# Expert stage of a Perceiver block: activation transposes three turns, second products four turns behind the row transposes, weights asked for three turns ahead

## What is computed

```python
logits = x @ router_w.T + expert_bias
top_w, top_idx = jax.lax.top_k(sigmoid(logits), 8)        # 160 experts, 2048 tokens
top_w = top_w / (sum(top_w) + 1e-09) * 2.5
h1 = silu(einsum('th,eih->eti', x, w_gate))               # w_gate 160 x 128 x 256
routed = einsum('eti,ehi->th', h1 * combine.T, w_down)    # w_down 160 x 256 x 128
x = x + routed + silu(x @ w_gate_shared.T) @ w_down_shared.T
```

## Time and profile before

| | |
|---|---|
| median of 3 runs | 1385.31 us (1382.23 to 1386.63) |
| the profiled execution | 1384.27 us |
| its span, first to last instruction | 1381.1 us |
| mean granted clock of TensorE over the span | 0.954 |
| expert stage, first weight request to last scatter | 1005.9 to 1329.2 us of the span |

### The profile page before, as it was taken

How to read it: one execution, slowest core, us unless ns; L and a number is a source line. 1 busy time by engine, 2 the same in 40 slices (tenths; PEclk the granted TensorE clock), 3 DMA queues, 4 the chain that set the end, 5 groups by cost and what they waited for, 6 DMA issues and landing times.

```text
span 1381.1 us, 34814 instructions
## 1 busy us (share of the span) xinstructions
PE 1244.3 (90%) x11693; PEld 897.9 (65%) x11693; DVE 946.3 (69%) x2728; ACT 605.4 (44%) x1761; POOL 548.0 (40%) x717
## 2 busy tenths in 40 slices
PE   5999999999998689999999999997848999999946
PEld 3667667767766356767776767775636776667725
DVE  2477666666666436787778887777637777777737
ACT  2445555455454156667667677665301111111140
POOL 1011110101100101556666666656616776667730
PEclk8999999999999779999999999999979999999969
DMA  9322323233323000111122111113298899898659
GB/s 308 99 98 90 133 91 138 93 133 108 133 80 106 32 16 16 37 65 53 57 64 73 57 65 54 64 38 103 91 263 254 257 267 279 262 265 253 207 211 368
DMA packets 124879, 185.73 MB, mean 134 GB/s; under 512 B 23285, under 2 KB 90516, under 8 KB 122784
## 3 DMA queue, kind: packets, MB, share of 16 engines
q10 hardware_dynamic: 57376, 77.19, 17.6%
q1 hardware_dynamic: 51200, 71.66, 16.9%
q0 software_dynamic: 16128, 34.67, 7.1%
HBM read 190.88 MB, written 78.25 MB: 195 GB/s over the span
## 4 chain that ended last, share of the span: by engine, by line
PE 43%; ACT 5%; ACTq 5%; DMA 4%; DVE 4%; issue 4%; POOL 1%; SPq 0%; DVEq 0%; POOLq 0%
PE bank L1038 5%; PE bank L1063 5%; PE bank L485 4%; ACT ex L472 3%; PE bank L1023 3%; PE bank L457 3%; ACTq L951 2%; PE bank L663 2%; PE bank L525 2%; PE bank L592 2%; PE bank L614 2%; PE bank L240 2%; PE bank L256 2%; PE bank L1050 1%; PE bank L433 1%
## 5 line engine op out<-in xcount | busy, mean ns | idle before, releaser
L1073 POOL DMA_INDIRECT y_d<-y,xg x208 | 204.0, 981 | 121.1 <-DVE y L1069 85.2
L1043 ACT ACTIVATE ex<-bank 128x256 f32<-128x256 f32 x104 | 40.0, 384 | 278.6 <-PE bank L1038 118.3
L773 POOL DMA_INDIRECT xs_d<-xw,slot_id x128 | 134.3, 1049 | 30.2 <-issue 29.3
L472 ACT ACTIVATE ex<-bank,nmC 128x256 f32<-128x256 f32 x256 | 119.2, 483 | 14.2 <-DVE nmC L466 13.8
L1069 DVE COPY y<-bank 128x512 f32<-128x512 f32 x104 | 71.9, 691 | 70.5 <-PE bank L1063 63.4
L485 PE MATMUL bank<-ident,ex 128*128 128x128 f32 x512 | 79.2, 284 | 20.0 <-ACT ex L472 16.6
L485 PEld LDWEIGHTS bank<-ident,ex 128*128 128x128 f32 x512 | 61.8, 145 | 54.3 <-ACT ex L472 21.1
L1023 PE MATMUL bank<-ident,xg 128*128 128x128 f32 x416 | 70.0, 292 | 19.4 <-DMA xg<-xs_d 19.4
L466 DVE TENSOR_REDUCE nmC<-bank 128x2 f32<-128x512 f32 x128 | 82.8, 680 | 5.7 <-PE bank L457 4.8
L1337 POOL TENSOR_TENSOR stB<-stB,small 128x1 f32<-128x1 f32 x32 | 20.3, 634 | 165.3 <-DVE stB L1334 165.3
L1027 DVE COPY ex<-bank 128x512 f32<-128x512 f32 x104 | 71.5, 687 | 21.0 <-PE bank L1023 16.3
(11 more groups left out here) (393 smaller groups left out, 3314.1 us busy)
## 6 DMA issues: line engine op xcount, KB each, us to landing
xs_d<-zeros ACTq DMA_DIRECT2D x16, 1768.0 KB, 7.4
pTC<-in_wexp ACTq DMA_DIRECT2D x104, 256.0 KB
xg<-xs_d SPq DMA_DIRECT2D x310, 68.0 KB
cT<-in_ctx SPq DMA_DIRECT2D x32, 512.0 KB, 4.0
wh<-in_wexp ACTq DMA_DIRECT2D x52, 256.0 KB
cT<-in_wexp ACTq DMA_DIRECT2D x52, 256.0 KB
kTC<-in_wexp ACTq DMA_DIRECT2D x52, 256.0 KB
vvC<-in_wexp ACTq DMA_DIRECT2D x52, 256.0 KB
```

The source lines that it names most:

```text
L472: last = act.activation(ex[:, u, 256 * b:256 * b + 256], bank[hp][:, 256 * b:256 * b + 256], ACT.Exp, bias=nm[:, u, b:b + 1], accum_out=su ...
L773: pool.indirect_dma_start(out=xs_d, out_offset=bass.IndirectOffsetOnAxis(ap=slot_id[z][:, k:k + 1], axis=0), in_=xw[z][:, k, :], in_offset ...
L1073: pool.indirect_dma_start(out=y_d, out_offset=bass.IndirectOffsetOnAxis(ap=who, axis=0), in_=y[:, n, g, :], in_offset=None, bounds_check=l ...
```

## The change

FLIP falls from 4 to 3 and DOWN from 5 to 4, so `flip` and `down` of a double are written one pass earlier. A constant AHEAD of 3 replaces the distance of 2 between a pass and the weights that it asks for; pass 0 asks for the weights of doubles 2 and 3. The loop has 108 passes instead of 109. Buffers and rings keep their sizes.

```diff
--- before.py
+++ after.py
@@ -955,7 +955,7 @@
 
 
     pe, dve, act, pool, sp = nc.tensor, nc.vector, nc.scalar, nc.gpsimd, nc.sync
-    UP, FLIP, DOWN, WEIGHED, EARLY = 2, 4, 5, 12, 3
+    UP, FLIP, DOWN, AHEAD, WEIGHED, EARLY = 2, 3, 4, 3, 12, 3
     GATED = range(2, 7)
     FETCHED, RESULTS, HELD, RING_W = 16, 6, 4, 2 * DEEP
     ex, pT, xw, slot_id, w, xgT, (hidden, h), s_rows, s_table, s_w = rings
@@ -1112,8 +1112,10 @@
         for m in range(UNITS):
             rows_sp(m)
         for i in range(DOUBLES + DOWN):
-            if i + 2 < DOUBLES:
-                load(i + 2)
+            if i == 0:
+                load(2)
+            if i + AHEAD < DOUBLES:
+                load(i + AHEAD)
             if i == 1:
                 rows_act(2)
             if i < DOUBLES:
```

## The result

The changed kernel takes **1395.78 us** (median of 8 runs, 1392.61 to 1398.15) against 1385.13 (8 runs, 1381.75 to 1388.69): a ratio of **1.0067, 95% interval 1.0045 to 1.0090**. It is slower by more than 0.3%, and lies 4.1 us above the top of the predicted range. The profiled execution took 1396.12 us, its span is 1394.3.

The account below looks back on a forecast made before the run. The prediction took ACT's issuing of requests to pace the long stretch, TensorE living on a lead. Terms 3.0 + 1.0 - 1.4 - 1.3 + 0 = +1.3 us gave 1386.6 us, range 1382.0 to 1391.7.

Parts of the forecast that it names:

- What bounds the kernel: Long stretch: ACT, at 2.86 us a turn against TensorE's 2.69, is slower; TensorE runs down a lead of two turns.
- (1): Activation transposes one turn sooner: ACT's rate unchanged, lead lost once, 3.0 us; waits over 10 us, silus never over 1.3 late.
- (2): ACT's request order: both page-number reads in the same turn make ACT run dry in light turns, 1.0 us (bounds 0 and 3).
- Rival C: ACT's requests: more weights in flight bring three more long request waits, uncovered by lead; 4.9 us slower, 1390.2; chance 0.10.
- (3): Wait for a free slot before a weight load: at most 0.1 us, inside the bounds of (2).
- (4): Second products four turns behind: DVE's copy stays covered, TensorE waits for no rows, costed at nothing.
- (5): The end: one double less left after the last row transposes, -1.4 us, and a shorter scatter queue on POOL, -1.3 us.
- (6): The start: load(5) delays the first silu to about 1028.5, TensorE waits 3.7 us, absorbed by later transfer waits: 0.
- rival B: The start: the 3.7 us wait for the first silu is not absorbed, about 5 us, 1391.6; chance 0.13.
- Rival A: The start: earlier weights pay, three transfer waits of 4.5 us together go, 1382.1; chance 0.13.

Follow-up runs that it names:

- a1: Kernel before with FLIP 3 and DOWN 4 of the change, weights still asked for two turns ahead: 1385.62 us, ratio 0.9996.
- a3: Changed kernel with the weights' page numbers read one turn earlier, so ACT's two reads fall in alternate turns: 1390.61 us, 1.0032 to the kernel before.
- a4: Changed kernel with both reads of page numbers one turn earlier, still paired but in odd turns: 1391.28 us, 1.0038 to the kernel before.
- a2: Kernel before with only the weights asked for three turns ahead, FLIP 4 and DOWN 5 kept: 1386.90 us, ratio 1.0007.
- c1: Changed kernel with 32 idle transposes on TensorE ahead of the loop, on a slower chip: 1.0160 to the kernel before.
- d3: Changed kernel with 32 idle transposes on TensorE ahead of the loop, measured again on a slower chip: 1.0172 to the kernel before.
- e1: Changed kernel with 32 idle transposes on TensorE ahead of the loop, once more on a slower chip: 1.0152 to the kernel before.
- b2: Kernel before with ACT reading 16 page numbers every fourth turn instead of 8 every second, on a slower chip: 0.9996 to the kernel before.
- f1: Kernel before with only the weights asked for three turns ahead, on a slower chip: 1.0022 to the kernel before.

## Why the prediction was wrong, step by step

**What bounds the kernel.** The reading that ACT is the slower engine and TensorE runs on a lead held: ACT's time adds up to the stretch in both kernels, the changed stretch is slower, not faster, than 2.86 us a turn, and the medians of ACT's requests did not move. Starting a DMA is not small here beside the DMA: a row request of 68 KB takes 0.48 us to issue, and at the 261 GB/s of the earlier trace rows its bytes are 0.27 us of the transfer engines' time, an estimate from these rows; no trace tells when these transfers landed. That ACT relieved alone would speed up the first chip could not be tried there.

**(1) Lead.** The price of the lead is right, and the end pays it back. Waits for ACT are 13.4 us (over 10 forecast). From silu 96 to the last silu the changed kernel takes 2.6 us more (3.0 forecast), from there to the last y copy 1.4 less (1.4), and the scatter follows 1.5 sooner (1.3). Together they should give +0.3: a1 gives +0.2, the changed kernel -0.2. But one sign of (1) failed: silus were never to be over 1.3 us late. The silu at 1262.63 comes 3.0 us after its first products ended (1258.92 + 0.71 = 1259.63), and 20 of the 84 are over 1.3 us late. In total a1 is at 0.9996, between 2.6 us faster and 1.7 slower.

**(2) Pairing of the reads: wrong by its size.** Silu intervals alternate by 3.60 - 2.36 = 1.24 us (1.2 forecast), but ACT ran dry for 3.1 us more, not 1.0, at the upper bound of 3. I stepped the intervals of the trace of before, in which only 13 were light. I stepped it without the meetings; each of these makes the long turn longer and TensorE wait, and the short turn after it can end no sooner than its first products (the interval of 1.95 above). How much of the 3.1 us comes that way I can't separate: a3, with neither pairing nor many meetings, has 1.3, and a4, with pairing and half the meetings, 2.7.

**The assumption that failed is in (1): "The rate of ACT does not change".** It did: the meetings rose from 3.3 to 10.8 us, 7.5 of the 9.0 us by which the stretch grew; dry gives 3.1, and the rest, reads of page numbers mostly, -1.6. Against the forecast these two are the miss: the forecast put 0 for the first and 1.0 for the second. Rival C had the symptom, single requests of over 1.2 us that are no longer covered, with three of them and 3.6 us. Its cause, "a turn more of weights in flight", is refuted by a2, which has that turn more in flight and 1.4 us of meetings. What brings the meetings, as the traces show them, is where ACT stands in its own order when a fetch comes. Fetches come every fourth turn of TensorE. In the kernel before ACT's place drifts against TensorE's, so they fall anywhere in its interval. In the changed kernel ACT is held close to TensorE, and 16 of the 21 fetches begin 2.5 to 3.4 us after the same silu of the four, at the end of the long turn, on the last weight requests and the row request behind them; four more begin within 0.5 us after the next silu. Being held close is not what costs: a1 holds ACT as closely, 16 of its 21 fetches begin 1.8 to 3.0 us after that same silu, and its meetings are 1.4 us. That a1 is free is thus partly luck of where its fetches fall. The one run on the first chip that moved the turn with the reads against the fetches, a4, halved the meetings; moving the fetches themselves was tried three times (c1, d3, e1) on chips where it could not show, and stays open.

**(3) Slot wait** (at most 0.1): in the kernel before, the changed kernel, a1 and a2 no gap of ACT of over 0.25 us in the stretch ends with the slot's semaphore. **(4)**: TensorE waits for no row between 1050 and 1300, so the cover held. **(5) End:** 3.8 us from the last y to its scatter, 4.3 at most forecast; the term was right. **(6) Start:** first silu at 1029.17 (1028.5 forecast), wait 3.53 us (3.7), transposes at 1029.61 (1029); turn 10 at 1049.66, 1.05 us later than taken, which is just past the 1049.5 from which rival B was to decide. B's price of 5 us did not come: silu 13 is 1.6 us late. Rival A, and with it the rule of the Trainium skill (DMA: Bandwidth & Descriptors, Rules for kernel authors) to issue early and wait late, was put to the test alone in a2: no weight is waited for, and the time is the same, 1.0007 [0.9991, 1.0022]; at the start a wait of 4.0 us for the first silu takes the place of one of 1.6 us for weights.

**Not foreseen at all:** the 2.8 us behind the last scatter, where TensorE's mean granted clock is 0.74 against 0.79 in the same stage before, and its 100 matmuls take 30.5 us against 27.6. The kernel before there:

```profile
1329.20:1381.10 51.90, 27.63 (x100) 21.77 (x100) 34.34 (x85) 15.99 (x53) 0.00 (x0) 0.79 0.90 364
```

The clock alone does not set that stage: in a2 it is 0.75 there, and the stage takes 51.9 us as before.

Of the 11.9 us between the profiled executions, then, 9.0 lie in the stretch; single profiles of a1 and a2 also put silu 13 and the last scatter 2 to 3 us later than before at equal medians, so I read nothing into 1 or 2 us of these.

The chances were wrong in one way that the working shows. I had costed each part at its own effect. a1 and a2 show each to be free on the first chip; the 10 us belong to the pair. My explanation, which fits a3 and a4, is that one takes away the cover under which the other was free.

## What to carry to other kernels

When one engine is slower than another and only a lead hides its unevenness, cost a change of the lead and a change of the unevenness together: on the first chip each alone came to less than 0.1%, both at once to 0.7%. Before shortening a distance between engines, list the longest single instructions of the slower engine, not its mean: here 1.2 to 1.5 us against a cover of 0.86. And measure such a change on more than one chip: taking out one turn of distance cost nothing on one, and 1.7% on another.

## What the runs showed of the hardware

A DMA request of ACT took over 1 us only where it overlapped an instruction packet of 16 KB that took 0.9 to 1.4 us: all 18 such requests in the stretch over the six traces of the first chip, and all 20 in the traces of the slower ones. On the first chip each of them ended 0.24 to 0.45 us after the packet. Reads of page numbers take 0.55 us for eight and 1.02 us for sixteen. On the first chip the kernel before took 1385 to 1386 us; in the five later sets of runs it took 1488 to 1501, with silu 13 to 96 in 307 us instead of 238 in b2, with register moves of 29 ns on ACT and SP that now and then take up to 0.93 us (f1), and TensorE stopping for up to 1.4 us amid first products. On chips of this kind the changed kernel itself was measured once, 1.6% slower; with idle transposes added, on three such chips, it was 1.5 to 1.7% slower.
